# Head sums of a recurrent unit as two one-pass products, the pieces of a step in another order, and six attention tiles moved forward

## The chip, the cores and the metric

One core of one Trainium2 chip runs the whole program in one launch. Times are device microseconds of one execution. TensorE is called PE, VectorE DVE, ScalarE ACT, GpSimd POOL, SyncE SP; POOL and SP do hardly anything here but issue transfers. A matmul's operands in 32-bit floating point are called fp32; fp32r is the same 32-bit word in which only a rounded value is kept, and which PE takes in a cheaper form of matmul.

## The reference, cut to what matters

`x` is 4 x 512 x 512 (batch, tokens, channels). It goes through three recurrent layers (RWKV form, 32 heads of 16 channels) and then one cross attention layer with 16 heads over 1024 context tokens. Of a recurrent layer:

```python
xa = _ln(x, ln1_w, ln1_b)
sx = concatenate([state[:, 1:2] - xa[:, :1], xa[:, :-1] - xa[:, 1:]], axis=1)
xxx = tanh((xa + sx * maa_x) @ maa_w1) ...          # five mixtures of xa and sx
w, r, k, v, g = ...                                 # five streams from the mixtures
def step(s, rkvw):
    a = k_t[..., :, None] * v_t[..., None, :]
    out = einsum('bhi,bhij->bhj', r_t, u * a + s)
    return a + w_t[..., :, None] * s, out
x1 = x + groupnorm(out) * g @ Wo.T
xc = _ln(x1, ln2_w, ln2_b)                          # then the feed-forward part
x = x1 + sigmoid(xr2 @ Wfr.T) * (square(relu(xk2 @ Wfk.T)) @ Wfv.T)
```

The attention layer norms the context (its audio_kv), projects Q, K and V, applies a mask and a softmax, and adds tanh(gate) times the projected output to `x`.

## The kernel before, in words

**Units and steps.** A recurrent layer of one batch and one half of its tokens is a unit: 3 layers x 2 halves x 4 batches give `ITS` = 24 units. A unit lies in SBUF as 128 partitions (channels) x 4 x 256 tokens. The loop over `s` (from -1 to `ITS`+1) is a software pipeline: in step `s` the code works at four units at once, `n = s+1` (norm, mixtures, streams v, k, r, g), `b = s` (recurrence: leaves of 8 tokens, then a scan over leaves), `c = s-1` (output product, second norm) and `e = s-2` (feed-forward part). Steps 2 to 22 have all four parts. The order of the pieces is written out by hand, once for each engine; each engine runs its own list strictly in that order, and semaphores tie the lists together.

**Head sums.** Inside a leaf, outputs need the dot product of r and k over the 16 channels of a head, for nine pairs of tokens (`P0a`, `P0b`, `P1`, `P2a`, `P2b`, `P4a` to `P4d`). DVE writes the elementwise product (a factor tile, 128x512), PE multiplies it with `blk` (128x128, ones in blocks of 16), which sums over a head and spreads the sum to its 16 channels, and DVE multiplies the result with v (`values`) and adds it up (`gather`). That is the fp32 matmul of `sum_heads`, nine per unit.

**PSUM rings.** PSUM's 8 banks are rings: `a_ring` (3 banks, unit n), `b_ring` (2 banks, unit b: head sums, transposes `VT`, `KT`, state updates `U`), `o_ring` (1), `c_ring` (2, units c and e). A tile may be filled when the tile that is one ring length earlier has been emptied. The tile lists (`A_TILES` to `C_TILES`) have to follow the order of the code.

**Transfers.** POOL loads the eight 1 MB weights of a step into three slots, each load once the last product with the slot's old weight has finished (`last_tile`). SP moves v into a masked layout `v_m` by four DMAs before each pair of updates (`load_vm`): those for pair 1 are issued when tile `U03` is full, and `U10` waits for them. Then come 16 DMAs that turn a unit's own output (`load_own`), the store of unit e and loads.

**Around the end.** Tiles of the attention's batch 0 are mixed into the last steps (`FIRST`): the context's norm (`mean0` to `rstd1`), `k00`, `k01`, `q0` (projections for head group 0) and `v0` to `v4`. A batch has 64 turns (4 groups x 4 blocks of 128 tokens x 4 heads); `BESIDE` says behind which turn a tile of this or the next batch is computed. In a turn PE makes the scores of a head (two fp32r matmuls of 512 columns), DVE adds the mask and takes the maximum, ACT takes exponentials, PE turns 8 pieces of the result of three turns earlier, and each fourth turn multiplies with V (`weighted`). Projections of k and q are split by ACT (`first_part`, rounded) and DVE (`second_part`, the rest).

Of the kernel before, what the change touches and what calls it, by code (L numbers as in the profile page):

```python
# [6 lines left out]
F32 = mybir.dt.float32  # L7
F32R = mybir.dt.float32r
U8 = mybir.dt.uint8
ALU = mybir.AluOpType  # L10
# [62 lines left out]
FIRST = ["mean0", "mean1", "var", "q0", "rstd0", "rstd1", "k00", "k01"] + [f"v{n}" for n in range(5)]  # L73
PARTS = ["q0", "k00", "k01"] + [f"{w}{e}{n}" for e in range(1, KT) for w, n in (("k", 0), ("k", 1), ("q", ""))]


def beside(n):
    if not 0 <= n < HEADS:
        return []
    b, turn = n // (TT * KT * HPT), n % (TT * KT * HPT)  # L80
    return [(b + off, name) for off, name in BESIDE.get(turn, ()) if 0 <= b + off < B]
# [28 lines left out]
B_TILES = [("P0a", "dve"), ("P0b", "dve"), ("P1", "dve"), ("P2a", "dve"), ("P2b", "dve"), ("VT0", "act"), ("VT1", "act"), ("KT0", "act"), ("KT1", "act"), ("P4a", "dve"), ("P4b", "dve"), ("P4c", "dve"), ("P4d", "dve"), ("U00", "act"), ("U01", "act"), ("U02", "act"), ("U03", "act"), ("U10", "act"), ("U11", "act"), ("U12", "act"), ("U13", "act")]  # L110
O_TILES = [("O0", "dve"), ("O1", "dve")]

C_TILES = [(2, "fr0", "act"), (2, "fr1", "act"), (2, "fk0", "act"), (1, "wo0", "dve"), (1, "wo1", "dve"), (2, "fk1", "act"), (1, "s1", "act"), (2, "fv0", "dve"), (2, "fv1", "dve"), (1, "m1", "dve"), (1, "s2", "act"), (1, "i1", "dve")]
# [4 lines left out]
LEAF_DVE = ["p0", "p1", "u1w", "u1r", "u1k", "p2a", "p2b", "u2w", "u2r", "u2k", "o1", "o2a", "p4a", "p4b", "p4c", "p4d", "u8", "u4r", "u4k", "o2b", "o4a", "o4b", "o4c", "o4d"]  # L118
STATE_ACT = ["d0", "s0", "carry0", "d1", "s1", "rz", "sq0", "std0", "carry1", "sq1", "aff0", "std1", "aff1"]
STATE_DVE = ["scan0", "own0", "scan1", "own1", "sum0", "mean0", "cen0", "var0", "rc0", "norm0", "back0", "sum1", "mean1", "cen1", "var1", "rc1", "norm1", "back1", "og0", "og1"]  # L120
# [3 lines left out]
F_ACT = ["kk0", "kk1"]  # L124

CONSTS = 12


def laid_out():
# [13 lines left out]
    for i in range(4):  # L143
        at[f"pr{i}"] = (at["mix1"][0] + 512 * i, 512)
# [1860 lines left out]
```

## Time and profile before

| | |
|---|---|
| median of 3 runs | 3205.1 us (3204.63 to 3209.02) |
| profiled execution, its own time | 3201.94 us |
| its span | 3200.2 us |
| busy share PE, DVE, ACT, POOL | 96%, 73%, 57%, 7% |
| PE's mean granted clock | 0.986 of 2.4 GHz |
| HBM traffic | 84 GB/s over the span |

The span is the time from the first to the last instruction; the execution's own time has 1.7 us more around it. "Busy" counts instructions that do work, not waits; matmuls overlap, so the busy time of a group of them is less than count times mean. In the chain of work that ended last, followed back from the last instruction, PE has 87%, DVE 7%, ACT 4%.

### The profile page before, as it was taken

The numbers are of one execution on the slowest core, as the hardware profiler recorded it, in microseconds if no ns is written. First come the engines' busy times: TensorE is split into PE (matmuls) and PEld (weight loads), VectorE is DVE, ScalarE is ACT, GpSimd is POOL, SyncE is SP. The second block draws the span as 40 slices with busy tenths as digits, with TensorE's granted clock in tenths as the row PEclk, the third lists the DMA queues.
The fourth block names the chain that finished last, engine by engine and source line by source line (L and its number), as shares of the span: only waits on it lengthen the run. The fifth ranks groups of instructions, "written<-read, shape, count | busy, mean of one in ns | idle before, by whom it ended". The sixth has DMA issues, their size and how long they took to land.

```text
span 3200.2 us, 77104 instructions
## 1 busy us (share of the span) xinstructions
PE 3063.3 (96%) x32684; PEld 2287.3 (71%) x32684; DVE 2338.7 (73%) x3819; ACT 1808.8 (57%) x3311; POOL 226.9 (7%) x457
## 2 busy tenths in 40 slices
PE   6899999999999999999999999997998998998998
PEld 4667777777777777777777777775665665665666
DVE  3788788887888787887887788876377566566566
ACT  3556555565655555555556555555366556556555
POOL 0000000000000000000000000000110101111010
PEclk8889999999999999999999999998999999999999
DMA  3223333343333333344333333343334224234131
GB/s 132 65 89 126 126 107 127 108 153 132 126 126 126 126 105 129 108 148 137 126 119 133 122 104 129 107 174 116 106 80 108 56 66 108 65 84 104 41 80 41
DMA packets 110357, 349.41 MB, mean 109 GB/s; under 512 B 22848, under 2 KB 56256, under 8 KB 84032
## 3 DMA queue, kind: packets, MB, share of 16 engines
q0 software_dynamic: 39936, 234.91, 23.2%
q1 hardware_dynamic: 69648, 106.28, 10.5%
q8 instruction: 262, 4.29, 0.6%
q10 hardware_dynamic: 432, 3.28, 0.3%
q14 instruction: 79, 0.65, 0.1%
HBM read 252.11 MB, written 16.78 MB: 84 GB/s over the span
## 4 chain that ended last, share of the span: by engine, by line
PE 87%; DVE 7%; ACT 4%; issue 1%; DMA 1%; SPq 0%; ACTq 0%; DVEq 0%
PE psum L734 42%; PE psum L743 6%; PE psum L901 5%; PE psum L919 4%; PE psum L871 3%; PE psum L800 3%; PE psum L861 3%; PE psum L784 3%; PE psum L891 3%; DVE psum L1727 2%; PE psum L876 2%; PE psum L687 2%; PE psum L699 2%; PE psum L867 1%; PE psum L667 1%; DVE mem L1732 1%
## 5 line engine op out<-in xcount | busy, mean ns | idle before, releaser
L734 PE MATMUL psum<-rw 128*128 128x256 f32 x6144 | 1402.8, 384 | 9.0 <-DVE rw L1529 5.4
L734 PEld LDWEIGHTS psum<-rw 128*128 128x128 f32 x6144 | 1155.1, 191 | 218.9 <-issue 54.0
L1727 DVE CUSTOM_DVE_ANT_0 psum<-psum,mem 128x1024 f32<-128x1024 f32 x256 | 313.6, 1225 | 77.3 <-PE psum L891 77.2
L1271 ACT ACTIVATE rest<-psum,mem 128x1024 f32<-128x1024 f32 x256 | 285.1, 1114 | 89.5 <-DVE mem L1727 87.8
L1523 DVE SCALAR_TENSOR_TENSOR rw<-psum,rw 128x256 f32<-128x256 f32 x480 | 196.0, 475 | 144.8 <-PE psum L700 79.5
L1183 ACT ACTIVATE rw<-psum,own 128x256 f32<-128x256 f32 x384 | 214.5, 714 | 123.7 <-PE psum L784 123.5
L901 PE MATMUL psum<-ident,rest 128*128 128x128 f32 x2048 | 270.4, 275 | 2.7 <-DVE mem L1686 1.6
L1624 DVE TENSOR_TENSOR_SCAN rw<-rw 128x2112 f32<-128x2112 f32 x48 | 217.4, 4529 | 70.6 <-ACT rw L1176 69.1
L901 PEld LDWEIGHTS psum<-ident,rest 128*128 128x128 f32 x2048 | 235.2, 141 | 42.3 <-issue 14.7
L1919 POOL DMA_DIRECT2D rw<-big_dram x192 | 101.7, 531 | 2157.2 <-PE psum L734 2124.3
L1264 ACT ACTIVATE mem<-psum 128x512 f32<-128x512 f32 x256 | 152.1, 595 | 141.0 <-PE psum L901 141.0
L743 PE MATMUL psum<-rw 128*128 128x512 f32 x432 | 217.3, 621 | 15.2 <-ACT rw L1144 7.9
L891 PE MATMUL psum<-side 128*128 128x512 f32 x512 | 211.2, 493 | 12.7 <-ACT rest L1271 10.3
L1732 DVE COPY mem<-psum 128x512 f32<-128x512 f32 x256 | 175.9, 687 | 36.7 <-PE psum L901 36.7
L1075 ACT ACTIVATE rw<-rw 128x256 f32<-128x256 f32 x192 | 99.9, 592 | 178.5 <-DVE rw L1471 178.5
L1934 POOL DMA_DIRECT2D side<-mem x256 | 123.8, 492 | 732.1 <-DVE mem L1703 615.3
L1611 DVE TENSOR_TENSOR rw<-psum,rw 128x512 f32<-128x512 f32 x168 | 116.0, 691 | 75.9 <-PE psum L743 70.7
L1140 ACT ACTIVATE rw<-psum 128x512 f32<-128x512 f32 x192 | 108.5, 591 | 64.1 <-PE psum L734 63.3
L919 PE MATMUL psum<-mem 128*32 128x128 f32 x4096 | 127.0, 277 | 16.9 <-DVE mem L1732 15.5
L1529 DVE TENSOR_TENSOR rw<-rw 128x1024 f32<-128x1024 f32 x120 | 143.1, 1211 | 0.0
L743 PEld LDWEIGHTS psum<-rw 128*128 128x128 f32 x432 | 77.8, 194 | 86.4 <-issue 61.5
L891 PEld LDWEIGHTS psum<-side 128*128 128x128 f32 x512 | 84.0, 190 | 75.4 <-issue 43.6
(157 smaller groups left out, 4297.4 us busy)
## 6 DMA issues: line engine op xcount, KB each, us to landing
rw<-big_dram POOLq DMA_DIRECT2D x192, 1024.0 KB, 5.6
side<-mem POOLq DMA_DIRECT2D x256, 128.0 KB, 4.1
rw<-xs_dram SPq DMA_DIRECT2D x32, 512.0 KB, 3.8
side<-mem SPq DMA_DIRECT2D x256, 64.0 KB, 2.0
rw<-rw SPq DMA_DIRECT2D x192, 64.0 KB, 2.0
rw<-rw SPq DMA_DIRECT2D x384, 32.0 KB
xs_dram<-rw SPq DMA_DIRECT2D x24, 512.0 KB, 6.4
rw<-x_dram SPq DMA_DIRECT2D x16, 512.0 KB, 5.0
```

What stands on the lines that cost most here:

```text
L734: last = mm(t[:, o * TC:(o + 1) * TC], big[:, k, P * m:P * m + P], src[:, k, 0:TC], start=k == 0, stop=k == KT - 1, skip_group_check=True)
L743: b_ring.fill(mm(t, blk, src, start=True, stop=True), it, name)
L891: last = mm(t[:, sh, :], q_side[group % 2][:, h, P * q:P * q + P].bitcast(F32R), k_side[group % 2][:, h, sh * 512:sh * 512 + 512].bitcast( ...
L901: last = nc.tensor.transpose(tokens(t, o), tokens(probs[:, n % HPT, :], first + o), ident[:])
L919: last = mm(t[AD * h:AD * h + AD, 0:P], v, probs_t[:, st, h, :], start=st == 0, stop=st == ST - 1, skip_group_check=True)
L1183: last = f(to[:, h], t[:, h], ACT.Identity, scale=own2[:, h:h + 1])
L1264: t_ring.empty(f(probs_t[:, 0:4, n % HPT, :], t.rearrange("p (s t) -> p s t", s=4), ACT.Copy), n, "t")
L1271: s_ring.empty(f(probs[:, n % HPT, :].rearrange("p (a s) -> p a s", a=2), s_ring.bank(n, "s"), ACT.Exp, scale=-1.0, bias=mx[:, n % 8:n % 8 ...
L1523: last = stt(to[:, m, :], t[:, o * TC:(o + 1) * TC], par(layer, MAAS, KT * FAN[s] + m), sxa[:, m, :], ALU.add, ALU.mult)
L1624: state_dve.inc(nc.vector.tensor_tensor_scan(s_flat[pair], d_flat, s_flat[pair], 0.0, ALU.mult, ALU.add), it, f"scan{pair}")
L1727: maxima.inc(nc.vector.tensor_tensor_reduce(t, t, mbias.rearrange("p (a s) -> p a s", a=2), 1.0, 3.4e38, ALU.add, ALU.min, accum_out=mx[:, ...
L1732: d_ring.empty(nc.vector.tensor_copy(probs_t[:, 4:8, n % HPT, :], t.rearrange("p (s t) -> p s t", s=4)), n, "t")
```

## The change

Each head sum becomes two fp32r matmuls that add up in one PSUM bank: `blk_r` (the block matrix, stored rounded) times the rounded factor tile, and `blk_r` times what the rounding left. ACT writes the rounded tile (`rounded`), DVE the rest (`remainder`); there are two buffers of each (`high`, `low`), so the rounding of a tile waits until the product two tiles earlier has finished. The factor tiles now lie in the three `mix` buffers. The factors of `P0a`, `P0b` and `P1` are computed at the end of the step before (`level0`, `products1`), those of P2 and P4 by `products2` and `products4`. The lists of all three engines are in another order: among others the `P` tiles stand between other products one by one, `spread_queries` and `scan_inputs` of the first pair are earlier on ACT, ACT empties `U12` and `U13` directly behind `scan_inputs(b, 1)`, and PE has only `v0` and `decay_in` between `updates(b, 0, 1)` and `updates(b, 1, 0)`. Tiles `v5`, `v6`, `v7` of batch 0 are computed at the end of step 24, `k10`, `k11`, `q1` at the end of step 25 and not beside turns 0, 1, 2, 4, 6 and 8; `q0` moves from the end of step 23 into step 24. `add4` is gone (`pick4` does its work).

```diff
-          39: [(1, "sum0"), (1, "sum1")], 41: [(1, "mean0"), (1, "mean1")], 46: [(1, "var")], 48: [(1, "q0")], 50: [(1, "rstd0"), (1, "rstd1")], 53: [(1, "k00")], 54: [(1, "k01")],
+          39: [(1, "sum0"), (1, "sum1")], 41: [(1, "mean0"), (1, "mean1")], 46: [(1, "var")], 50: [(1, "rstd0"), (1, "rstd1")], 53: [(1, "k00")], 54: [(1, "k01")], 55: [(1, "q0")],
-FIRST = ["mean0", "mean1", "var", "q0", "rstd0", "rstd1", "k00", "k01"] + [f"v{n}" for n in range(5)]
+FIRST = ["mean0", "mean1", "var", "rstd0", "rstd1", "k00", "k01", "q0"] + [f"v{n}" for n in range(ST)] + ["k10", "k11", "q1"]
...
+        def factors(it, name):
+            n = SUMS.index(name) % 5
+            slot = mix[(STREAMS * it + (2, 0, 1)[n // 2]) % 3].rearrange("p k t -> p (k t)")
+            return slot[:, 512 * (n % 2):512 * (n % 2) + 512]
...
-            def sum_heads(it, name, src):
+            def products(it, name):
+                if (it, name) == (0, "P0a"):
+                    pe.wait_ge(blk_rounded, 1)
+                pe.wait_ge(low_dve.sem, low_dve.at(it, name))
+                n = SUMS.index(name) % 2
                 t = opened(b_ring, it, name)
-                b_ring.fill(mm(t, blk, src, start=True, stop=True), it, name)
+                mm(t, blk_r[:].bitcast(F32R), high[n].bitcast(F32R), start=True, stop=False)
+                b_ring.fill(mm(t, blk_r[:].bitcast(F32R), low[n].bitcast(F32R), start=False, stop=True), it, name)
...
+            def rounded(it, name):
+
+                act.wait_ge(leaf.sem, leaf.at(it, name.lower()))
+                n = SUMS.index(name)
+                if n >= 2:
+                    act.wait_ge(b_ring.full, b_ring.full_at(it, SUMS[n - 2]))
+                elif it:
+                    act.wait_ge(b_ring.full, b_ring.full_at(it - 1, SUMS[-1]))
+                high_act.inc(f(high[n % 2].bitcast(F32R), factors(it, name), ACT.Copy), it, name)
...
+            def remainder(it, name):
+                dve.wait_ge(high_act.sem, high_act.at(it, name))
+                n = SUMS.index(name)
+                low_dve.inc(tt(low[n % 2].bitcast(F32R), factors(it, name), high[n % 2].bitcast(F32R).bitcast(F32), ALU.subtract), it, name)
```

PE's list of a full step, in its new order (the first line of each engine's loop and all conditions left out):

```
fr0, s1(n), fr1, P0a, m1(n), P0b, fk0, P1, s2(n), P2a, wo0, VT0, VT1, i1(n), P2b, P4a, fk1, P4b, wo1,
KT0, KT1, lora(n), P4c, P4d, lora_three 0, fv0, lora_three 1, U00, U01, s1(c), fv1, lora_sum, m1(c),
U02, U03, v0, decay_in, U10, U11, decay_out, v1, lora_two 0, U12, U13, lora_two 1, k0, s2(c), k1, i1(c),
O0, r0, O1, r1, g0, g1
```

DVE's list at the end of step 25, where unit 23's output is finished:

```diff
                 if has_e:
                     norm_c(e, "mixk")
...
+                if s == ITS + 1:
+                    after(0, "k10")
...
+                if s == ITS + 1:
+                    after(0, "k11")
+                    after(0, "q1")
...
+                if has_e:
+                    unit_out(e, 0)
...
+                if has_e:
+                    unit_out(e, 1)
...
                 if s == ITS + 1:
                     mask_bias(0)
```

## Rows read from the trace of the kernel before

**Rows 1.** The page: span, and busy time, share and instructions of each engine.

```profile
span 3200.2 us, 77104 instructions
PE 3063.3 (96%) x32684; PEld 2287.3 (71%) x32684; DVE 2338.7 (73%) x3819; ACT 1808.8 (57%) x3311; POOL 226.9 (7%) x457
```

**Rows 2.** Windows: us; busy PE, PEld, DVE, ACT, POOL; granted clock, DMA share, GB/s.

```profile
74.90:160.90 86.00, 69.31 (x840) 49.90 (x841) 64.77 (x103) 42.83 (x79) 2.12 (x4) 0.88 0.23 77
160.90:248.90 88.00, 82.67 (x977) 61.66 (x976) 70.75 (x112) 48.72 (x92) 2.65 (x5) 0.91 0.26 89
1059.70:1149.70 90.00, 89.66 (x1041) 70.11 (x1040) 72.82 (x115) 51.99 (x97) 4.23 (x8) 1.00 0.37 124
2141.00:2220.90 79.90, 61.64 (x782) 41.41 (x781) 52.74 (x70) 35.61 (x60) 2.11 (x4) 0.87 0.45 161
2220.90:2299.50 78.60, 75.86 (x355) 54.04 (x353) 24.09 (x37) 28.84 (x52) 9.85 (x20) 1.00 0.35 101
```

**Rows 3.** PE in order of time, a full step: start, us, line, count [idle before].

```profile
1059.69 1.88 PE L743 MATMUL psum<-rw 128*128 128x512 f32 x4
1061.40 3.62 PE L734 MATMUL psum<-rw 128*128 128x256 f32 x16
...
1082.34 1.98 PE L743 MATMUL psum<-rw 128*128 128x512 f32 x4
1084.25 1.14 PE L687 MATMUL psum<-rw 32*128 32x256 f32 x12
...
1092.77 3.72 PE L734 MATMUL psum<-rw 128*128 128x256 f32 x16
...
1100.62 1.15 PE L784 MATMUL psum<-rw 32*32 32x128 f32 x64
1101.71 1.09 PE L713 MATMUL psum<-rw 128*64 128x128 f32 x16
```

**Rows 4.** PE in order of time, attention: two fp32r score matmuls, four turns.

```profile
2340.89 0.71 PE L891 MATMUL psum<-side 128*128 128x512 f32 x2
2341.44 1.04 PE L901 MATMUL psum<-ident,rest 128*128 128x128 f32 x8
...
2350.31 0.71 PE L891 MATMUL psum<-side 128*128 128x512 f32 x2
```

**Rows 5.** Groups of instructions, DVE, one full step: line, count, busy, mean ns, idle before.

```profile
L1523 DVE SCALAR_TENSOR_TENSOR rw<-psum,rw 128x256 f32<-128x256 f32 x20 | 8.2, 480 | 5.2 <-PE psum L700 2.6 <-PE psum L687 2.5
```

**Rows 6.** DVE and ACT in order of time: operations of 128x512.

```profile
1120.86 0.60 ACT L1140 ACTIVATE rw<-psum 128x512 f32<-128x512 f32 x1
...
1145.65 0.69 DVE L1562 TENSOR_TENSOR rw<-rw 128x512 f32<-128x512 f32 x1
1146.25 0.69 DVE L1564 TENSOR_TENSOR rw<-rw 128x512 f32<-128x512 f32 x1
```

**Rows 7.** The line of load_vm's DMAs, one step and a half: from issue to landing.

```profile
L484 SPq DMA_DIRECT2D rw<-rw x9: 593/606/707, 1076.7 to 1166.4; - x9
DMA to landing us min/median/max: 1.9/2.0/5.5
```

**Rows 8.** PE in order of time, from step 23 to turn 4 of the attention.

```profile
2182.02 1.15 PE L784 MATMUL psum<-rw 32*32 32x128 f32 x64 [2.55 <-DMA rw<-rw]
2183.11 5.41 PE L734 MATMUL psum<-rw 128*128 128x256 f32 x16
...
2201.88 2.33 PE L800 MATMUL psum<-rw 128*32 128x32 f32 x128 [6.17 <-ACT rw L1155]
...
2269.22 7.13 PE L871 MATMUL psum<-mem 128*128 128x512 f32 x16
2276.19 13.98 PE L734 MATMUL psum<-rw 128*128 128x256 f32 x64
...
2299.56 0.70 PE L891 MATMUL psum<-side 128*128 128x512 f32 x2 [0.87 <-DVE rw L1679]
...
2312.57 0.70 PE L891 MATMUL psum<-side 128*128 128x512 f32 x2
```

More of the change, by code:

```diff
@@ L80, in beside @@
     b, turn = n // (TT * KT * HPT), n % (TT * KT * HPT)
-    return [(b + off, name) for off, name in BESIDE.get(turn, ()) if 0 <= b + off < B]
+    return [(b + off, name) for off, name in BESIDE.get(turn, ()) if 0 <= b + off < B and (b + off or name not in FIRST)]
 def turned_tiles():
@@ L124 @@
 F_ACT = ["kk0", "kk1"]
[L126 removed]
+SUMS = ["P0a", "P0b", "P1", "P2a", "P2b", "P4a", "P4b", "P4c", "P4d"]
+HIGH_ACT = list(SUMS)
+LOW_DVE = list(SUMS)
+CONSTS = 11
 def laid_out():
     at, n = {}, 0
[L132 removed]
+    for name, size in [("blk_r", P), ("pick4", P), ("pars", LAYERS * PARS), ("s_first", KT * B * 32), ("s_now", KT * B * 32),
                        ("first_edges", 2 * KT * B), ("half_edges", 2 * 2 * KT * B), ("small_w", SMALL)] + [(f"slot{i}", SLOT) for i in range(NSLOT)] + [
@@ L843, in batch_tile @@
                     pe.wait_ge(*d_ring.empty_at(b, f"sum{sh}"))
-                    last = mm(t, add4[:], sums(b)[:, 512 * sh:512 * sh + 512], start=True, stop=True)
+                    last = mm(t, pick4, sums(b)[:, 512 * sh:512 * sh + 512], start=True, stop=True)
                 elif name[:4] == "mean":
@@ L953, in _ @@
                     values_by_token(b)
+                if 0 < n and has_n:
+                    norm_a(n, "i1")
+                if has_b:
+                    products(b, "P2b")
+                    products(b, "P4a")
+                if has_e:
+                    feed(e, "fk", 1)
+                if has_b:
+                    products(b, "P4b")
                 if has_c:
@@ L968, in _ @@
                     lora_three(n, 0)
+                if has_e:
+                    feed(e, "fv", 0)
+                if has_n:
+                    lora_three(n, 1)
+                if has_b:
+                    updates(b, 0, 0)
+                if has_c:
+                    norm_c(c, "s1")
+                if s == ITS:
+                    batch_tile(0, "q0")
+                if has_e:
+                    feed(e, "fv", 1)
+                if has_n:
+                    lora_sum(n)
+                if has_c:
+                    norm_c(c, "m1")
+                if has_b:
+                    updates(b, 0, 1)
+                if has_n:
+                    stream(n, "v", 0)
+                    decay_in(n)
                 if s == ITS - 1:
@@ L1789, in _ @@
                 if has_b:
+                    products4(b, 3)
+                    values(b, "P2b", 0, 2, 1)
+                    values(b, "P4a", 1, 4, 0)
+                    gather(b, "P2b", "o2b", 0, 2)
+                    remainder(b, "P4b")
                     level4(b)
@@ L1819, in _ @@
                     mixed(n, "w")
+                    mixed(n, "v")
+                if s == ITS:
+                    after(0, "q0")
+                if has_b:
+                    gather(b, "P4d", "o4d", 0, 4)
+                if has_e:
+                    unit_out(e, 1)
+                if has_c:
+                    norm_c(c, "m1")
+                if has_b:
+                    scan(b, 0)
+                if s == ITS + 1:
+                    mask_bias(0)
                 if s == ITS - 1:
```

406 lines of the change are left out of this document (206 added, 200 removed).

## The prediction

> **What bounds the kernel now.** First the page and the windows, whose five stretches are step 0, step 1, a full step, step 23, and steps 24 and 25. PE is busy for 96% of the span [rows 1], and in a full step, 90.0 us long, for 89.66 us, while DVE is busy for 72.82 and ACT for 51.99 us [rows 2]. So steps 2 to 22 are as long as PE's list, and what shortens that list shortens the step, until another engine or a wait takes over. Steps 0 and 1 are different: PE is busy for 69.31 of 86 and 82.67 of 88 us at a granted clock of 0.88 and 0.91 [rows 2]; part of them is set by DVE. Step 23 has no next unit and leaves PE idle for 18 of 79.9 us; in steps 24 and 25 PE works for 75.86 of 78.6 us again [rows 2]. Then PE and DVE in order of time: there the reader sees what each piece costs on its engine, from one start to the next, which is fairer to overlapping matmuls than their own durations.
>
> **Head sums on PE.** Two fp32 sums cost 1061.40 - 1059.69 = 1.71 us ahead of a projection and 1084.25 - 1082.34 = 1.91 us ahead of small products [rows 3]; all nine of this step add up to 8.29 us, that is 0.92 each. The trace has no fp32r sum that adds two products, but the two score matmuls have its shape: 128x512, two in a row, each with its own weights. They cost 2341.44 - 2340.89 = 0.55 us there [rows 4]. That is one bound; the other is half of the cheapest fp32 sum, 0.43 us. I take 0.53, near the row of the same shape, as most sums will stand alone between other products. Saved: 0.92 - 0.53 = 0.39 us, times nine = 3.5 us a step (3.3 and 4.4 by the bounds). PE's floor is then 90.0 - 3.5 = 86.5 us.
>
> The same price by a rule: the Trainium skill ("TensorE: Matmul & The Clock Gate", section "Back-to-back issue gap") gives 215.7 ns for an isolated warm matmul of 512 columns and about 131 ns in a sustained stream. By the first the pair would cost 0.43 us and a step would lose 4.4 us, by the second still more; the row above, 0.55 for two, bears out neither.
>
> **The new work beside it.** DVE gets nine `remainder`s of 128x512. Independent ones follow each other by 1146.25 - 1145.65 = 0.60 us [rows 6]: 5.4 us a step, so that DVE has 72.8 + 5.4 = 78.2 us of work in 86.5. ACT gets nine roundings of the same size, 0.6 us each by an ACT copy of that size [rows 6], 5.4 us; 57 of 86.5. Both are hidden in sum. What can fail is the order, since each engine's list is strict: with 8.3 us left, DVE may not wait much. Now it idles for 90.0 - 72.8 = 17.2 us, 5.2 us of it ahead of the mixtures alone, for PE's small products [rows 5].
>
> I walked the three new lists once with these durations, counting from the start of `fr0`. DVE's necessary waits come to 1.7 us before the first scan (`U03` full at 45.8, emptied by ACT at 48.2), 3.5 before the `w2r0` mixture (PE reaches it at 57.2), 0.4 before `w2r1` and about 1 in small ones: 6.6 us, with 78.2 makes 84.8 of 86.5. The joints at which PE needs DVE soon after it is ready are `lm` (28.9, wanted at 29.1), the rest of `P4b` (23.9 for 24.1), `m1` (DVE free at 8.6, tile full at 8.9), and the reciprocal for `i1(c)` behind the second scan (67.3 for 67.2). None is late by more than 0.2; I charge 0.2 us a step for them, from 0 to 1.5, since an error of 1 us in a chain of 55 us of DVE work is easy.
>
> **The transfer into `v_m`.** `load_vm` for pair 1 starts when `U03` is full and `U10` waits for it. Now PE has 1100.62 - 1092.77 = 7.85 us of other work between them [rows 3]; afterwards only `v0` and `decay_in`, about 3.6 + 1.1 = 4.7 us [rows 3]. SP needs 3 x 0.6 = 1.8 us until the last of the four is issued, which lands 1.9 to 5.5 us later [rows 7]: 3.7 to 7.3 us in all. The long landings are those beside two weight loads that start together; in the new order one weight load (slot free when `fv1` ends, 2 us before) is in flight, not two. I take 5.0 us, a wait of 0.3 us; the bounds are 0 and 2.6. Behind the waiting `U10` on PE stand `td2` and everything after it, and DVE's second scan behind those, so it adds to the step in full.
>
> A full step is thus 86.5 + 0.2 + 0.3 = 87.0 us, 3.0 less. Steps 2 to 22 and the sums of step 23 make 22 x 3.0 = 66 us. In steps 0 and 1 DVE's extra 5.4 us lies partly on the path, but the first factors are computed ahead; I take 3 us less for both (from 5 less to 4 more).
>
> **The end.** Three groups of edits meet.
> First, the tiles: each is eight fp32 matmuls of 512 columns; the two from 2269.22 to 2276.19 cost 7.0 us, so three cost 10.4 [rows 8]. `v5` to `v7` now stand ahead of `fr0` of unit 23, where `v3` and `v4` already fill the wait: 10.4 us more. `k10`, `k11`, `q1` stand behind `fv1`: 10.4 more. And DVE's list has their `second_part`s ahead of `unit_out(23)`, which empties the bank that the scores want: after `q1` come 0.85 on ACT and 0.7 + 2.1 on DVE, 3.7 us with the starts, against 0.87 now [rows 8]: 2.8 more. In return the attention starts without tiles. Turn 4 comes 2312.57 - 2299.56 = 13.0 us after turn 0 now [rows 8]; without tiles I get 8.3 by the chain score, maximum, exponential over two banks, the mask's 1.4 us included. From turn 4 to 16 it takes 37.7 us now (2350.31 - 2312.57), and four turns without a tile take 2350.31 - 2340.89 = 9.4 us [rows 4], so 28.3. Together 10.4 + 10.4 + 2.8 - 4.7 - 9.4 = 9.5 us more: turns without a tile are set by DVE, so tiles were half hidden there, and PE has no room for them in steps 24 and 25.
> Second, `q0`: 3.5 us more in step 24.
> Third, step 23: `O0` waits 6.17 us for `spread_queries`, which ran behind other ACT work [rows 8]; it now runs early, ACT empties `U12` and `U13` about 4 us sooner, and the context's squares stand ahead of the group norm. I get `fr0` of step 24 10 us earlier, 3.5 of them `q0`'s own. Bounds 4 and 14.
> Sum of the end: 9.5 + 3.5 - 10 = +3 us, between -5 and +12.
>
> **Sum.** 3201.9 (the profiled execution's own time) - 66 - 3 + 3 = 3136 us. The median shown is 3.2 us above that execution, so 3139 us.
>
> **Rivals.**
> *A, PE alone sets the step.* Joints and transfer cost nothing and the pair costs 0.48, between its bounds: 22 x 4.0 = 88, with 5 less in steps 0 and 1 and 3 less at the end, 3205 - 96 = 3109 us. For it: DVE has 1.7 us to spare; against: the transfer's gap shrinks from 7.85 to 4.7 us. Chance 0.22.
> *B, DVE's list sets the step.* If its waits shrink only from 17.2 to about 10.3 us, a step is 88.5: 22 x 1.5 = 33, and 3205 - 33 + 3 = 3175 us. For it: the waits of [rows 5] are on tiles that PE finishes late in the list; against: the walk, in which the P4 factors fill such gaps. Chance 0.15.
> *C, slower.* The transfer is late by 2.5 us or more. Where `U` waited 2.55 us for it in step 23, the 16 matmuls behind took 5.41 us and not 3.72 [rows 8], half speed for a while. A step would then lose 3.5 us and get back 2.5 + 1.7 + 0.2 = 4.4: 22 x 0.9 = 20, with the end's 3, 3228 us. It decides from a lateness of about 2 us. Against it: 7.2 us would be needed for what I put at 5.0, near the longest of [rows 7]. Chance 0.05. The Trainium skill ("TensorE: Matmul & The Clock Gate", section "What's actually happening") has the clock fall to half after idleness; by that rule the many small joints of a step could do the same, and the row at 2182.02 shows the drop itself. But steps 24 and 25 have PE idle for 2.7 us in pieces of about 1 us at a clock of 1.00 [rows 2, 8], so small waits alone don't do it.
> *D, the change doesn't do what it says.* If the rounded pair cost as much per matmul as fp32, a step would grow by 8.3 us; the pair of [rows 4] excludes it nearly. Chance 0.01.
>
> **How the numbers follow.** My forecast (3115 to 3165) has 0.57. Of cases and their fringes 0.92 lie below 3198.7, 0.2% under the median (about what this kernel's measurement can tell from no change), 0.02 within it, 0.06 above. The range 3106 to 3178 holds A's and B's centres and leaves C, D and the outer halves of A and B.
>
> **What the profile after would show.** The line of the sums with two records per sum as now, but of about 0.27 us each from start to start; a step of 87.0 us, PE busy for all but half a microsecond; DVE's idle time down to 9 us; a short wait of `U` for the DMA in most steps. Turn 0 of the attention about 52 us earlier (69 + 10 - 3.5 - 20.8 - 2.8) and turn 16 about 66 us. Wrong would be: a step under 86.3 or over 88.5 us, waits of PE on `remainder` in each step, a granted clock under 1.00 in the full steps, or an end that costs over 12 us.

## The result, and the profile after

| | median | lowest to highest | ratio to the kernel before, 95% interval |
|---|---|---|---|
| before | 3204.86 us | 3199.83 to 3209.02 | |
| changed | 3148.22 us | 3145.25 to 3154.74 | 0.9827 [0.9809, 0.9844] |
| changed, second series | 3148.12 us | 3146.95 to 3150.47 | 0.9831 [0.9817, 0.9845] |

The change saves 57 us. The forecast was 3139 us: right in sign and within the range, 9 us too low. The rows below are from the changed kernel's first profiled execution, which took 3154.74 us itself and so lies 6.5 us above the median.

The page after, span and engines [rows 1]. PE has 65 us less work, DVE 118 and ACT 159 us more.

```profile
span 3153.0 us, 77916 instructions
...
PE 2998.3 (95%) x32684; PEld 2298.9 (73%) x32684; DVE 2456.3 (78%) x4034; ACT 1967.3 (62%) x3550; POOL 226.3 (7%) x457
```

The windows after, in the stretches of [rows 2]: step 0, step 1, a full step, step 23, steps 24 and 25. The third row is a full step in which nothing waits: 86.2 us, PE busy for 86.13 of them. The forecast had 86.5 for PE's floor and 78.2 and 57 us for DVE and ACT; the row has 77.73 and 58.73.

```profile
74.90:155.10 80.20, 67.27 (x842) 50.63 (x838) 64.17 (x103) 46.45 (x86) 2.13 (x5) 0.83 0.22 74
155.10:247.80 92.70, 80.81 (x981) 63.10 (x977) 78.81 (x128) 57.37 (x105) 3.02 (x6) 0.89 0.26 92
865.80:952.00 86.20, 86.13 (x1043) 70.00 (x1041) 77.73 (x125) 58.73 (x108) 4.23 (x8) 1.00 0.38 130
2084.80:2155.10 70.30, 54.63 (x774) 40.81 (x774) 55.66 (x75) 41.72 (x69) 2.11 (x4) 0.87 0.48 176
2155.10:2260.80 105.70, 100.87 (x412) 65.73 (x410) 25.21 (x39) 33.55 (x62) 9.83 (x20) 0.98 0.26 75
```

PE in order of time in that full step, against [rows 3]. L764 and L765 are the two products of a head sum. From start to start the first takes 0.42 us here (870.65 to 871.07) and 0.34 at 877.56, the second 0.33 and 0.22; the first of these sums costs 0.75 in all, the second 0.56, and one that follows another sum 0.47 (878.12 to 878.59).

```profile
870.65 0.59 PE L764 MATMUL psum<-parts,blk_r 128*128 128x512 f32 x1
871.07 0.40 PE L765 MATMUL psum<-parts,blk_r 128*128 128x512 f32 x1
871.40 0.65 PE L642 MATMUL psum<-rw,ones 128*32 128x64 f32 x32
...
877.56 0.50 PE L764 MATMUL psum<-parts,blk_r 128*128 128x512 f32 x1
877.90 0.39 PE L765 MATMUL psum<-parts,blk_r 128*128 128x512 f32 x1
878.12 0.40 PE L764 MATMUL psum<-parts,blk_r 128*128 128x512 f32 x1
878.36 0.39 PE L765 MATMUL psum<-parts,blk_r 128*128 128x512 f32 x1
878.59 3.62 PE L751 MATMUL psum<-rw 128*128 128x256 f32 x16
```

DVE's groups in that step, against [rows 5]: the mixtures wait 4.5 us (5.2 before), the scans 1.6 (forecast 1.7).

```profile
L1699 DVE TENSOR_TENSOR_SCAN rw<-rw 128x2112 f32<-128x2112 f32 x2 | 9.1, 4555 | 1.6 <-ACT rw L1220 1.6
L1584 DVE SCALAR_TENSOR_TENSOR rw<-psum,rw 128x256 f32<-128x256 f32 x20 | 8.2, 477 | 4.5 <-PE psum L717 4.3 <-PE psum L704 0.2
```

Not every step is like that one. Measured from one `P0a` to the next, steps 2 to 21 have a mean of 87.50 us (90.17 before). PE's waits in them (engine and line, releaser, us in total, times, longest): `U10` (L799) waits for the transfer into `v_m` in 12 places; the list of the kernel before had no such wait of PE in these steps.

```profile
PE psum L799 <- DMA rw<-rw: 11.0, 12, 1.4
PE psum L815 <- issue: 3.4, 3, 1.7
PE psum L751 <- issue: 2.7, 2, 2.0
```

What such a wait can bring with it: PE in order of time in step 4, and the window behind the wait (the clock is the first number behind the POOL column). Behind a wait of 1.38 us the 16 matmuls of `v1` take 4.97 us where 3.72 is usual, at a granted clock of 0.72, and step 4 is 89.3 us long.

```profile
466.25 1.15 PE L799 MATMUL psum<-rw 32*32 32x128 f32 x64 [1.38 <-DMA rw<-rw]
467.33 1.54 PE L740 MATMUL psum<-rw 64*128 64x128 f32 x16
468.80 4.97 PE L751 MATMUL psum<-rw 128*128 128x256 f32 x16
```

```profile
468.00:474.00 6.00, 6.00 (x28) 4.76 (x26) 0.10 (x1) 5.16 (x14) 0.00 (x0) 0.72 0.20 54
```

PE in order of time from step 23 to turn 16, against [rows 8]. `O0` (L815) no longer waits 6.17 us; the sums of the second norm (L642, L648) wait 3.09 and 3.53. `rstd0` (L870) waits 3.34 us for the reciprocal on DVE (L1765). Turn 0 waits 3.48 us for `unit_out` (L1754), turn 4 follows 8.47 us later and turn 16 37.2 us after turn 0.

```profile
2122.38 1.15 PE L799 MATMUL psum<-rw 32*32 32x128 f32 x64 [2.29 <-DMA rw<-rw]
2132.99 0.65 PE L642 MATMUL psum<-rw,ones 128*32 128x64 f32 x32 [3.09 <-ACT rw L1096]
2137.18 1.08 PE L648 MATMUL psum<-rw,pick 128*32 128x64 f32 x32 [3.53 <-DVE rw L1529]
2141.45 0.75 PE L815 MATMUL psum<-rw 128*32 128x32 f32 x31 [1.06 <-DVE rw L1714]
2151.64 3.75 PE L870 MATMUL psum<-mem,pick 128*128 128x256 f32 x8 [3.34 <-DVE mem L1765]
```

```profile
2260.80 2.04 PE L906 MATMUL psum<-side 128*128 128x512 f32 x4 [3.48 <-DVE rw L1754]
...
2269.27 1.15 PE L906 MATMUL psum<-side 128*128 128x512 f32 x2
...
2297.98 0.71 PE L906 MATMUL psum<-side 128*128 128x512 f32 x2
```

In the kernel before, `q0` (L867) stood between `var` and `rstd0` (L855), and `rstd0` had no wait:

```profile
2214.83 3.67 PE L867 MATMUL psum<-mem 128*128 128x512 f32 x8 [0.29 <-DMA mem<-xs_dram]
2218.33 1.03 PE L855 MATMUL psum<-mem,pick 128*128 128x256 f32 x4
```

The span cut at five marks; us against the kernel before. The marks are `P0a` of steps 2 and 23 (before 248.97 and 2141.01; after 247.79 and 2084.85) and turns 0 and 16. The second execution is that of the second series, span 3147.0.

| stretch | forecast | first execution | second |
|---|---|---|---|
| start to step 2 | -3 | -1.2 | -3.2 |
| steps 2 to 22 | -63 | -55.0 | -59.3 |
| `P0a` of step 23 to turn 0 | +14.1 | +17.4 | +17.7 |
| turns 0 to 16 | -14.1 | -13.6 | -13.5 |
| turn 16 to the end | 0 | +5.1 | +5.1 |
| sum | -66 | -47.2 | -53.2 |

Two rows ask for an explanation: the full steps, and a stretch of the attention on which the forecast had nothing.

### The profile page after: what moved, and what is told of

It reads as the page before. It is cut to its first block, busy times and chain, and to the rows that moved or that the text cites. A ratio compares the mean times of both kernels' runs of the same rounds, so it can differ in the third digit from the quotient of the medians.

```text
span 3153.0 us, 77916 instructions
## 1 busy us (share of the span) xinstructions
PE 2998.3 (95%) x32684; PEld 2298.9 (73%) x32684; DVE 2456.3 (78%) x4034; ACT 1967.3 (62%) x3550; POOL 226.3 (7%) x457
## 3 DMA queue, kind: packets, MB, share of 16 engines
q1 hardware_dynamic: 69648, 106.28, 10.9%
## 4 chain that ended last, share of the span: by engine, by line
PE 86%; DVE 8%; ACT 2%; DMA 2%; issue 1%; SPq 1%; ACTq 0%; DVEq 0%
PE psum L751 42%; PE psum L916 5%; PE psum L934 4%; PE psum L886 4%; PE psum L799 3%; PE psum L876 3%; PE psum L815 3%; PE psum L906 3%; DVE psum L1802 3%; PE psum L764 2%; PE psum L891 2%; PE psum L882 2%; PE psum L704 2%; PE psum L765 2%; PE psum L716 2%; DMA rw<-rw 1%
## 5 line engine op out<-in xcount | busy, mean ns | idle before, releaser
L751 PEld LDWEIGHTS psum<-rw 128*128 128x128 f32 x6144 | 1161.2, 192 | 212.9 <-issue 43.1
L1181 ACT ACTIVATE parts<-rw 128x512 fp32r<-128x512 f32 x216 | 133.9, 622 | 37.5 <-PE psum L765 21.6
L1624 DVE TENSOR_TENSOR parts<-rw,parts 128x512 fp32r<-128x512 f32 x216 | 147.0, 681 | 0.4 <-ACT parts L1181 0.4
L934 PE MATMUL psum<-mem 128*32 128x128 f32 x4096 | 128.5, 279 | 17.7 <-DVE mem L1807 16.2
L934 PEld LDWEIGHTS psum<-mem 128*32 128x32 f32 x4096 | 111.4, 112 | 36.9 <-DVE mem L1807 21.0
```

The lines of the kernel that those rows point to most:

```text
L751: last = mm(t[:, o * TC:(o + 1) * TC], big[:, k, P * m:P * m + P], src[:, k, 0:TC], start=k == 0, stop=k == KT - 1, skip_group_check=True)
L934: last = mm(t[AD * h:AD * h + AD, 0:P], v, probs_t[:, st, h, :], start=st == 0, stop=st == ST - 1, skip_group_check=True)
L1624: low_dve.inc(tt(low[n % 2].bitcast(F32R), factors(it, name), high[n % 2].bitcast(F32R).bitcast(F32), ALU.subtract), it, name)
```

## The experiments

Each is the changed kernel with one edit, except where several are named. The cuts show the lines that matter; waits and counters that follow from them are left out. Times are medians; what is compared within a few us stands against the changed kernel at 3148.

**The order without the products: fp32 sums in the new order.**

```diff
-                mm(t, blk_r[:].bitcast(F32R), high[n].bitcast(F32R), start=True, stop=False)
-                b_ring.fill(mm(t, blk_r[:].bitcast(F32R), low[n].bitcast(F32R), start=False, stop=True), it, name)
+                b_ring.fill(mm(t, blk_r[:], factors(it, name), start=True, stop=True), it, name)
```

> The changed kernel, its order, its roundings and rests, but each head sum is one fp32 product of the unrounded factor tile, as in the kernel before; the rounded value and the rest are computed and not used. Theory T (TensorE's list sets the step): a step is longer by 9 x (0.92 - 0.59) = 3.0 us and the wait for v_m stays: 90.5 us a step, 3148 + 22 x 3.0 = 3214 us. Rival R (much of the gain came from the order, not from the cheaper products): 3160 to 3185 us.

3226.57 us (3224.56 to 3229.19), ratio to before 1.007 [1.0057, 1.0082]. DVE and ACT still make the two parts. PE in order of time, two `P0a` one step apart:

```profile
891.71 1.02 PE L764 MATMUL psum<-rw,blk_r 128*128 128x512 f32 x2
...
981.38 1.02 PE L764 MATMUL psum<-rw,blk_r 128*128 128x512 f32 x2
```

A step without a wait is 89.7 us here and 86.2 with the products: 3.5 us for nine sums, 0.39 each, exactly the term of the forecast. It also shows that everything else in the change (the order, the moved tiles, the making of the parts) makes the kernel 22 us slower, and that the cheaper products are worth 78 us, 12 more than the theory, which took 0.33 us a sum. The 22 us are not in the steps without a wait, which are 0.3 us shorter than before (89.7 against 90.0). Between the two profiled executions, 25 us apart, 4.0 us lie before step 2, 11.4 in steps 2 to 22, where `U10` waits for the transfer, and 9.9 from `P0a` of step 23 on.

**Only the rounded product.** The rest is neither made on DVE nor multiplied, so this leaves out part of each head sum.

```diff
-                mm(t, blk_r[:].bitcast(F32R), high[n].bitcast(F32R), start=True, stop=False)
-                b_ring.fill(mm(t, blk_r[:].bitcast(F32R), low[n].bitcast(F32R), start=False, stop=True), it, name)
+                b_ring.fill(mm(t, blk_r[:].bitcast(F32R), high[n].bitcast(F32R), start=True, stop=True), it, name)
```

> Changes the computation: each head sum is only the product of the rounded value; the rest is neither made on VectorE nor multiplied. Theory (TensorE's list sets a full step): nine second products of 0.17 to 0.24 us go, a step without a wait falls from 86.2 to 84.1 to 84.7 us, and with 20 such steps the time from 3148 to 3105 to 3118. Rival (VectorE's or ScalarE's order sets the step by now): VectorE loses nine operations of 0.6 to 0.7 us, so a step could fall to about 80 to 82 us if it were what set it, but TensorE's own work forbids less than 84; what tells it is where TensorE waits: under the rival waits on VectorE stand in the steps of the changed kernel and not here. If the products were hidden already: 86.2 as before.

3110.12 us (3108.97 to 3113.12), ratio 0.9708 [0.9694, 0.9723]. The window of one step:

```profile
839.60:925.40 85.80, 84.57 (x1034) 68.55 (x1032) 72.43 (x115) 58.59 (x106) 4.24 (x8) 1.00 0.39 130
```

The step is 85.8 us, of which PE waits 0.92 for `v_m` and 0.21 for ACT, so 84.6 without waits: inside the theory's range. DVE loses 5.3 us of work and the step only 1.6, which are PE's. PE's list sets the step. The shorter step also has more of the transfer's waits, 13.6 us in 15 places.

**Each rest computed twice on DVE.**

```diff
+                tt(low[n % 2].bitcast(F32R), factors(it, name), high[n % 2].bitcast(F32R).bitcast(F32), ALU.subtract).then_inc(rest_once, 1)
+                dve.wait_ge(rest_once, len(SUMS) * it + n + 1)
                 low_dve.inc(tt(low[n % 2].bitcast(F32R), factors(it, name), high[n % 2].bitcast(F32R).bitcast(F32), ALU.subtract), it, name)
```

> Each rest is computed twice on VectorE, one behind the other with a wait between: nine more operations of about 0.65 us, 5.9 us a step; TensorE's list and ScalarE's are as in the changed kernel. Theory (the chains through VectorE have some slack, but less than its 8.5 us of idle time a step, since each sum's operations are spread over the step and joined one behind the other): the step becomes 1 to 5 us longer, the time 3170 to 3250. Rival (VectorE has 8.5 us of idle time a step and all of it can be used): under 0.5 us a step, the time under 3160.

3263.26 us (3259.56 to 3268.91), ratio 1.0181 [1.0164, 1.0198]: more than either side expected. The window of one step, and the wait of PE that is largest in sum in steps 2 to 21:

```profile
905.50:996.50 91.00, 87.49 (x1042) 69.66 (x1041) 83.50 (x134) 58.79 (x107) 4.24 (x8) 1.00 0.36 123
```

```profile
PE psum L765 <- DVE parts L1627: 64.0, 100, 1.0
```

DVE has 5.8 us more work (83.50 against 77.73) and the step without other waits is 4.8 longer (91.0 against 86.2). Of DVE's 8.5 us of idle time only about 1 us was to be had, near the walk's 1.7 us. The 4.8 us a step are inside the theory's range and the total is not: in the trace 8 us are lost before step 2 and 6 between `P0a` of step 23 and turn 0, which the theory had not counted. The changed kernel stands about one microsecond of DVE work before the point at which DVE's chain would set the step.

**A longer gap between `U03` and `U10`.**

```diff
+                if has_b:
+                    updates(b, 0, 1)
                 if has_n:
                     lora_sum(n)
                 if has_c:
                     norm_c(c, "m1")
-                if has_b:
-                    updates(b, 0, 1)
```

> The changed kernel with one edit: on TensorE the updates U02, U03 stand ahead of the sum and mean products (lora_sum, m1 of unit c) and not behind them, so that 5.8 us of other work and not 4.7 us lie between U03 and U10, which waits for the transfer into v_m. Theory T (the transfer is late in about half of the steps, by 0.3 to 2.3 us, and in four steps the clock falls to half behind it; together 1.3 us a step above the 86.2 us of a clean step): the mean of steps 2 to 21 falls from 87.5 to 86.3..86.7 us, the whole is 16 to 24 us faster than the changed kernel, that is about 3128 us. Rival R (the 1.3 us are VectorE's list or something else that only shows at these places): steps stay at 87.5, about 3148 us.

3147.71 us (3143.78 to 3154.78), ratio 0.9825 [0.981, 0.9841]: no gain, against the theory, although a step without a wait is 86.0 us here, 0.2 shorter. Waits of `U10`: 11.8 us in 13 places. The transfer's line and PE at that place, one step (issues: count, ns, first and last start; then us from issue to landing):

```profile
L501 SPq DMA_DIRECT2D rw<-rw x4: 601/758/1297, 1071.8 to 1074.4; - x4
...
DMA to landing us min/median/max: 3.1/3.6/4.3
```

```profile
1077.55 1.15 PE L799 MATMUL psum<-rw 32*32 32x128 f32 x64 [0.21 <-DMA rw<-rw]
```

In the changed kernel the same step has:

```profile
L501 SPq DMA_DIRECT2D rw<-rw x4: 594/603/996, 1077.0 to 1078.9; - x4
...
DMA to landing us min/median/max: 2.7/3.0/3.2
```

At this place the gap was 1.0 us longer, and from the first issue to `U10` it took 0.6 longer (5.8 us against 5.2), so that only 0.4 of the wait went. Over steps 2 to 21 the four transfers took, from first issue to last landing, a median of 5.8 us (5.3 to 7.2) against 5.1 (4.1 to 5.9) in the changed kernel. In both a 1 MB weight load had been issued shortly before on POOL, into the slot that `fv1` frees; in the new PE order `fv1` ends just ahead of `U03`. The edit brought the transfer nearer to that load: 0.9 us behind it and not 2.0. This gave the next experiment.

**The load beside the transfer issued later.**

```diff
                     tiles, name = last_tile[old]
+                    if old == WFV and old_it + 2 < ITS:
+                        tiles, name, old_it = b_ring, "U10", old_it + 2
                     pool.wait_ge(tiles.full, tiles.full_at(old_it, name))
```

> The load of the next 1 MB matrix into the slot that the fv product leaves free waits for U10 and U11, the products that read the v_m of the second pair: it is issued about 6 us later, behind the 4 small transfers of v_m and not beside them. The first run of this study issued those transfers 5 us earlier and they landed no sooner, with a 1 MB load beside them in either. Theory (the load beside them makes the v_m transfers land late: 3.1 us and more from issue to landing where 1.9 us is their quickest): the waits of U10 on DMA fall from 11.0 us in steps 2 to 21 to under 4, the four steps with half-speed stretches behind such a wait lose them, the mean of steps 2 to 21 goes from 87.5 to 86.4 to 87.0, the time from 3148 to 3134 to 3140; the matrix is next needed over 13 us after its new landing. Rival (the landing is set by the four issues on SyncE, one behind the other, and by when U03 ends): the waits stay at 9 us or more, the time at 3145 to 3150.

3131.83 us (3126.77 to 3133.57), ratio 0.9772 [0.9757, 0.9786]: 16 us less, 2 past the theory's range. First POOL's load in the changed kernel at the step shown above:

```profile
1074.96 0.53 POOL L2016 DMA_DIRECT2D rw<-big_dram  x1 [14.86 <-PE psum L751]
```

Then, with the edit: POOL, the transfer, PE's `U10`, and its waits in steps 2 to 21.

```profile
1071.77 0.53 POOL L2018 DMA_DIRECT2D rw<-big_dram  x1 [22.88 <-PE psum L799]
```

```profile
L501 SPq DMA_DIRECT2D rw<-rw x4: 594/602/832, 1065.8 to 1067.9; - x4
...
DMA to landing us min/median/max: 1.9/2.3/2.5
```

```profile
1070.32 1.15 PE L799 MATMUL psum<-rw 32*32 32x128 f32 x64
```

```profile
PE psum L799 <- DMA rw<-rw: 1.0, 3, 0.4
```

The load now starts 6.0 us behind the transfer and not 2.0 ahead of it; the landing falls from 3.0 to 2.3 us and `U10` waits no more. Over steps 2 to 21 first issue to last landing has a median of 4.1 us (3.8 to 4.9), and steps 2 to 21 go from 87.50 to 86.63 us, 17.4 us in all (13.4 against the second execution's mean of 87.30). Of the 17.4, 10.0 are waits for the transfer and 3.3 the time at the lower clock behind two of them: steps 4 and 5 are 3.1 and 2.9 us over 86.2, of which the waits are 1.38 and 1.32. Another 3.6 are probably not the edit's: in steps 6 and 19 PE stands for 1.7 to 2.0 us in both kernels with no releaser in the profile, and these steps are 90.0 and 89.8 us long in this execution of the changed kernel and 88.1 with the edit, but 88.9 and 87.9 in the changed kernel's second execution, and step 6 is 90.0 again in a version below that has this edit too. So the transfer's price is some 13.3 us in these steps; in step 23, outside them, `U10` waited 2.29 us and now waits 0.69. The Trainium skill ("DMA: Bandwidth & Descriptors", section "Issuing engines are not separate DMA queues") says that transfers started by SyncE, ScalarE and GpSimd end up on the same 16 DMA engines and interleave; the runs agree, with 64 KB transfers of SP slowed by a 1 MB load of POOL.

**`q0` of batches 1 to 3 back at turn 48.** `BESIDE` gets back its old entry, `FIRST`'s order for batch 0 stays.

```diff
-          ... 46: [(1, "var")], 50: [(1, "rstd0"), (1, "rstd1")], 53: [(1, "k00")], 54: [(1, "k01")], 55: [(1, "q0")],
+          ... 46: [(1, "var")], 48: [(1, "q0")], 50: [(1, "rstd0"), (1, "rstd1")], 53: [(1, "k00")], 54: [(1, "k01")],
```

> The changed kernel with q0 of batches 1 to 3 beside turn 48 and not 55. Theory T (at turn 48 it is half hidden behind VectorE, at 55 it adds to a run of tiles; the blocks of each batch differ by 1.7 us): 5 us faster than the changed kernel, about 3143 us. Rival R (the difference in the two traces was chance): 3148 us.

3141.06 us (3138.54 to 3143.03), ratio 0.9802 [0.9788, 0.9815]: 7 us less, where the theory had 5. In the trace, turn 0 to the end is 887.7 us, against 892.2 in both executions of the changed kernel and 900.6 before. PE in order of time at that place of the changed kernel: `k01` (L876), `q0` (L882) and `v0` (L886) follow each other with one turn between them, each 3 us and more of PE work. What `q0` costs is read from the turns' starts, the same in each of three batches. Turns 48 to 50 together take 11.1 us with `q0` and 9.0 without it: PE then waits 1.43 us for ACT before the scores of turn 49, which `q0` had covered. Turns 55 and 56 take 8.3 us without `q0` and 12.1 with it. So it costs 2.1 us at turn 48 and 3.8 at turn 55, 5.2 more in three batches.

```profile
2424.77 3.96 PE L876 MATMUL psum<-mem 128*128 128x512 f32 x6
...
2432.04 3.60 PE L882 MATMUL psum<-mem 128*128 128x512 f32 x8
2435.08 1.02 PE L906 MATMUL psum<-side 128*128 128x512 f32 x2
...
2437.12 3.27 PE L886 MATMUL psum<-mem 128*128 128x512 f32 x7
```

**The six tiles of batch 0 back beside the turns.** `v5` to `v7`, `k10`, `k11`, `q1` leave `FIRST` and steps 24 and 25, `q0` stays where the change put it.

```diff
-FIRST = ["mean0", "mean1", "var", "rstd0", "rstd1", "k00", "k01", "q0"] + [f"v{n}" for n in range(ST)] + ["k10", "k11", "q1"]
+FIRST = ["mean0", "mean1", "var", "rstd0", "rstd1", "k00", "k01", "q0"] + [f"v{n}" for n in range(5)]
```

> The changed kernel with v5, v6, v7, k10, k11, q1 of batch 0 beside turns 0, 1, 2, 4, 6, 8 again. Theory T (TensorE has no room for them in steps 24 and 25, and turns without tiles are set by VectorE): turn 0 comes 23 us earlier, turns 0 to 16 take 13.6 us more, net 10 us faster than the changed kernel, about 3138 us. Rival R (the tiles were free in the recurrent steps and cost at their turns): 5 to 20 us slower, 3153 to 3168 us.

3145.29 us (3142.85 to 3148.39), ratio 0.9818 [0.9804, 0.9831]: 3 us less, between the two. PE in order of time: a wait of 6.01 us in step 25 that the changed kernel does not have, and turn 0 with its old wait of 0.87.

```profile
2209.91 16.06 PE L751 MATMUL psum<-rw 128*128 128x256 f32 x64 [6.01 <-DVE rw L1518]
...
2235.36 0.70 PE L906 MATMUL psum<-side 128*128 128x512 f32 x2 [0.87 <-DVE rw L1735]
```

From `P0a` of step 23 to turn 0 there are 160.5 us, 15.5 fewer than with the tiles moved; turns 0 to 16 take 50.75 again, 13.6 more. So moving them costs 1.9 us net. The forecast priced PE's six tiles in full, with 2.8 for the wait of turn 0, against 14.1 saved, which is 9.5 net. What it had not seen is that three of the tiles now lie over a wait of 6 us for DVE. Without them the 64 matmuls behind that wait take 16.06 us where 13.98 is usual, at a granted clock of 0.51 for their first 4.1 us. With both, 20.8 + 2.6 - 6.0 - 2.1 makes 15.3 of the 15.5 us measured. And turn 0 to the end takes 905.7 us here, 5.1 more than before with the same tiles in it: `q0`'s price a second time.

**The last unit's x1 ahead of three evictions.** In step 25 DVE does `unit_out(23)` and the mask before `after(0, "k10")`, `"k11"` and `"q1"`.

```diff
-                if s == ITS + 1:
-                    after(0, "k10")
...
                 if s == ITS + 1:
                     mask_bias(0)
+                    after(0, "k10")
+                    after(0, "k11")
+                    after(0, "q1")
```

> In the last step VectorE does the last unit's x1 and the mask ahead of the second parts of k10, k11 and q1, which are three evictions. Theory: TensorE's wait of 3.48 us before the first scores is on that x1's queue, 2.6 us of it (the three evictions, or as far as they had stood ahead) goes: 3145 to 3146. Rival: the wait only moves, because turn 16's tiles or the first maxima need what is now evicted later: 3148, with a new wait of 2 to 3 us in the first 16 turns.

3142.77 us (3136.95 to 3145.16), ratio 0.9806 [0.9791, 0.982]: 5 us less, 2 more than the theory. The first turns:

```profile
2249.65 1.50 PE L906 MATMUL psum<-side 128*128 128x512 f32 x4
2254.12 0.73 PE L906 MATMUL psum<-side 128*128 128x512 f32 x2 [2.98 <-ACT rest L1308]
```

The 3.48 us are gone and turns 0 to 16 are no longer than before the edit (36.7 us), so no new wait took their place: the 2.98 us before turn 2 were 2.59 in the changed kernel. The median fell by 5.4. In the trace, `P0a` of step 23 to turn 16 is 4.9 us shorter (208.3 against 213.1), of which 4.1 lie between the start of `q1` and turn 0.

**Versions with several of these edits**, on one chip with the changed kernel.

The changed kernel itself first.

> The changed kernel as it is, beside the versions below, so that those of a few us apart are compared with it directly: 3145 to 3151, mean of steps 2 to 21 at 87.1 to 87.5 us.

3148.12 us; mean of steps 2 to 21 87.30 us, and in them 13.1 us of waits of `U10` for the transfer in 12 places.

The load behind `U10`, `q0` at turn 48 and the six tiles back, with the three diffs above:

```diff
+                    if old == WFV and old_it + 2 < ITS:
+                        tiles, name, old_it = b_ring, "U10", old_it + 2
...
+          ... 46: [(1, "var")], 48: [(1, "q0")], 50: [(1, "rstd0"), (1, "rstd1")], 53: [(1, "k00")], 54: [(1, "k01")],
...
+FIRST = ["mean0", "mean1", "var", "rstd0", "rstd1", "k00", "k01", "q0"] + [f"v{n}" for n in range(5)]
```

> Three edits of before in one: the load waits for U10, q0 of batches 1 to 3 is back at turn 48, and the six moved tiles of batch 0 are back in the attention. Theory (each acts in a place of its own, so they add): 16 us less for the load, 5 to 7 for q0 and 2 to 3 for the tiles: 3148 less 23 to 26, 3122 to 3125. Rival (the tiles or q0 gained only on their runs' clock, and the load alone counts): 3129 to 3132.

3126.09 us (3120.59 to 3126.25), ratio 0.9757 [0.9742, 0.9772]: 22 us less, 1 us short of the theory's range. No wait of `U10` for a DMA is left in steps 2 to 21.

The load behind `U10`, `q0` at turn 48, the tiles left where the change put them, and x1 ahead of three evictions:

```diff
+                    if old == WFV and old_it + 2 < ITS:
+                        tiles, name, old_it = b_ring, "U10", old_it + 2
...
+          ... 46: [(1, "var")], 48: [(1, "q0")], 50: [(1, "rstd0"), (1, "rstd1")], 53: [(1, "k00")], 54: [(1, "k01")],
...
                     mask_bias(0)
+                    after(0, "k10")
+                    after(0, "k11")
+                    after(0, "q1")
```

> The load waits for U10, q0 of batches 1 to 3 is back at turn 48, the six tiles stay in the last steps, and the last unit's x1 and the mask go ahead of three of their evictions on VectorE. Theory: 16 us, 5 to 7 and 3.5 (the wait before the first scores, which was gone in that run): 3148 less 24.5 to 26.5, 3121.5 to 3123.5, so with that wait gone the moved tiles cost no more than the same tiles put back. Rival (a moved tile costs its full time again, as the run with the tiles back had it by 2 to 3 us): 3125 or more, above the version with the tiles back.

3123.06 us (3117.69 to 3123.24), ratio 0.9748 [0.9733, 0.9763]: 25 us less, as the theory had it. With turn 0's wait gone the moved tiles cost 10.9 us ahead of turn 0 (169.0 against 158.1 from `P0a` of step 23), and from turn 0 to the end there are 884.95 us against 898.85. So, once turn 0's wait is gone, moved tiles beat tiles put back by 3 us, in the medians as in the traces; the two versions' runs overlap (3117.69 to 3123.24 and 3120.59 to 3126.25), so it rests on the traces.

The same with the longer gap:

```diff
+                if has_b:
+                    updates(b, 0, 1)
                 if has_n:
                     lora_sum(n)
                 if has_c:
                     norm_c(c, "m1")
```

> The same with U02 and U03 ahead of the lora sum and the normalisation's mean, 1.1 us more between U03 and U10. By itself this brought nothing, as the transfer ran beside the 1 MB load then. Theory: with the load out of the way all that is left of the waits of U10 (1.0 us in three steps, and one step of 88.1 with them) goes: 0.5 to 3 us under the version without it. Rival: the rest of the steps' spread is TensorE's clock and issue, not the transfer: the same within 1.5 us.

3119.33 us (3118.02 to 3120.37), ratio 0.974 [0.9726, 0.9753]: 3.7 us under the version without the gap, a little over the theory's range; steps 2 to 21 have a mean of 86.41 us (86.64). The waits of `U10` that were left, 0.9 us in all, are gone, but most of the gain is another: a step without a wait is 86.0 us in this order and 86.2 in the other, 4 us in 20 steps. The longer gap gave the same 0.2 us when it was tried alone, and there later landings took them back. PE's only waits in these steps are

```profile
PE psum L760 <- issue: 4.0, 3, 2.6
PE psum L824 <- issue: 1.3, 2, 1.2
```

This is the fastest version found, 29 us under the changed kernel and 83 under the kernel before.

## Why the prediction was right or wrong

**What bounds the kernel: right.** PE's list set the step before and sets it after. Less work on PE alone (only the rounded product) shortened the step by its own amount, and a step without a wait is 86.2 us where the forecast's floor was 86.5.

**Head sums on PE: right.** The saving of 0.39 us each was measured by putting fp32 sums back. A pair costs more than the 0.53 taken (nine from start to start add up to 5.35 us, 0.59 each), but the 16 matmuls ahead of a sum give some of it back: the sum at 870.65 and the projection ahead of it take 4.02 us together (from 867.38), the same two with an fp32 sum 4.40 (893.86 to 898.26 in that run), though the sums alone differ by only 0.75 against 0.95. The Trainium skill ("TensorE: Matmul & The Clock Gate", section "Back-to-back issue gap") has about 216 ns for an isolated matmul of 512 columns; the trace agrees for most products (0.22 to 0.24 us) and not for the first of a row of sums (0.34 to 0.42) nor for the last one ahead of small matmuls (0.32 to 0.33).

**DVE and ACT: right.** 77.7 and 58.7 us of work against 78.2 and 57, the waits ahead of scans and mixtures as walked, and no wait of PE on `remainder` in steps 2 to 21. The joints, charged at 0.2 us a step, cost nothing. Rival B did not come, but by about 1 us of DVE work, as the run with each rest twice showed.

**The transfer into `v_m`: mis-sized.** This is the term that failed most. The forecast took 0.3 us a step; the run with the load moved measured 0.67 (13.3 us in 20 steps, as worked out there). The time from `U03` to landing was about what was taken in the middle, a median of 5.1 us for 5.0, but it varies from 4.1 to 5.9, so that `U10` waited in 12 of 20 steps, and two waits of over 1.3 us were followed by a stretch at the lower clock. That is rival C's mechanism in small: it made steps 4 and 5 89 us long. The forecast had seen that a weight load is in flight and had counted on its being one and not two; it had not asked what the transfer would cost without it, which is 4.1 us. Another 0.3 us a step are stops of PE without a releaser (6.1 us in 20 steps), and 0.2 the lower clock behind them in steps 6 and 19, which the forecast did not have. 86.2 + 0.67 + 0.3 + 0.2 makes 87.4 of the measured 87.5, where the forecast had 87.0. It had also taken 90.0 us for the step before, whose mean was 90.17, and by that luck a third of this miss does not show in the saving.

**Steps 0 and 1.** -3 forecast, -1.2 and -3.2 measured.

**The end: errors that nearly cancel, and one that does not.** The 27.1 us from `fr0` of step 24 to turn 0 (10.4 + 10.4 + 2.8 + 3.5) were measured as +26.9 (78.68 to 105.61), and the turns' gain of 14.1 as 13.6. That the sum 27.1 came out was in part chance: with the tiles back this stretch is 89.5 us long, so the tiles cost 16.1 us for the forecast's 23.6 and `q0` and the order 10.8 for its 3.5, because of the wait of 6 us in step 25 which the tiles cover. Step 23 got 9.5 us shorter, not 13 (10, and 3 for its sums). What failed there is the forecast's "3.5 of them `q0`'s own": `q0` had filled the time in which `rstd0` waits for the reciprocal, and with `q0` gone `rstd0` waits 3.34 us. The second norm's sums wait 3.09 + 3.53 = 6.6 us where they waited 2.40 + 1.56 = 4.0 before; other waits of the step shrank.

**Overlooked: `q0` of the later batches.** The diff moves it from turn 48 to turn 55 for batches 1 to 3, next to `k00`, `k01` and `v0`. The forecast costed only batch 0's. By the rule it used itself (turns without a tile are set by DVE, so a tile there is half hidden) a tile set beside three others is not hidden. That is 5.1 us in the traces; undone it gave 4.5 in the trace and 7 in the medians.

Against the second execution the errors are 3.7 (full steps), 3.6 (step 23), 5.1 (`q0`) and 0.4 us from the other rows, 12.8 of 66. The medians differ by 56.6 us where these two executions' own times (3201.94 and 3148.79) differ by 53.2, so of the 12.8 about 9 are left between forecast and median. Two of the forecast's signs of being wrong did appear: the granted clock fell under 1.00 in full steps (behind the waits in steps 4 and 5), and the end, counted as the forecast counts it and with the three `q0`s, costs 12 us where it had 3.

## What to carry to other kernels

When an order is changed, ask for each transfer on the critical path not only how much work lies between issue and use, but which big load is released just before it: issuing one load behind the transfer and not ahead of it was worth 16 us here, and making the gap longer alone was worth nothing. A tile can stand in a wait that nobody sees while it is there: two waits, of 3.3 and 6 us, showed here only when a tile was taken away. When tiles are moved in a table that serves several batches, price the entry once for each batch, and look at what stands beside it in its new place. A reordering that makes cheap operations possible can cost by itself (22 us here, tiles moved with it included); a run of the new order with the old operations tells the two apart.

## What the runs showed of the hardware

- A transfer of 64 KB issued by SP lands in 1.9 us at its quickest and in 2.7 to 4.3 us at the two places shown beside a 1 MB load of POOL; in the kernel before, where two such loads start together, mostly 2.5 us ahead of it, the four of steps 2 to 21 took 4.3 to 7.3. An issue takes 0.6 us and now and then up to 1.9; that happens with the load moved away too (up to 1.7).
- The same wait of PE has two prices. Behind 1.38 and 1.32 us (steps 4 and 5) the next 16 matmuls took 4.97 and 4.55 us; behind 1.30 and 1.25 us (steps 7 and 8) 3.72. It is not the length alone: in the run with the longer gap, waits of 1.64 and 1.65 us were followed by 4.60 and 4.26 us, and two others of 1.63 and 1.65 by 3.72. The Trainium skill ("TensorE: Matmul & The Clock Gate", section "What's actually happening") ties the lower clock to idleness; the granted clock of 0.72 behind the first of them agrees, and the pairs show that waits of nearly one length fall on either side.
- PE stops for 1.0 to 2.6 us, with no releaser in the profile, 63 to 70 us behind `P0a` of steps 6 and 19 in every kernel in the new order but the one with only the rounded product, which stops in other steps. The traces hold a hint: in five of them each stop of over 0.7 us in steps 2 to 21 ends 2.2 to 2.9 us after the start of a 16 KB transfer of kind `instruction` (queue q8), with a next one 3.3 to 4.5 us behind it. Most such pairs have no stop between them (27 of 31 in the changed kernel), and no run was made to tell whether PE waits for its own instructions there.
